# The table of chunks ahead of the feature loads, biases loaded from ScalarE's queue, and side steps spread over a whole sum

## The reference, cut to what matters

```python
agg = segment_sum(h_src[src], dst); out = elu((agg * norm_dst) @ weight + bias)      # L0
h = relu(gcn_conv(x, ...)); z = h @ W_lin + b_lin                                    # L1
out = relu(z @ W_dec1 + b_dec1) @ W_dec2 + b_dec2
h = prelu(hconv(x, W1, b1)); h = prelu(hconv(h, W2, b2) + x)                         # L2
# hconv: xt = x @ W; m = segment_sum(xt[src], dst) * Binv; segment_sum(m[dst], src) * Dinv + b
x = m @ W_gc + b_gc + feats @ W_res + b_res; y = x + moe_ff(x)   # L3: top 2 of 64 experts
```

## Time and profile before

| | us |
|---|---|
| median of 3 runs (2074.12 to 2080.96) | 2080.48 |
| the profiled execution, its own time | 2079.78 |
| its span in the trace | 2078.0 |

### The profile page before, as it was taken

One profiled execution on the slowest core, in us unless ns is written; L12 is line 12 of the kernel. 1 busy time (PEld: TensorE's weight loads), 2 busy tenths in 40 slices (PEclk: granted clock), 3 DMA queues, 4 the chain that ended last, 5 costly groups with the idle time before them and its releaser, 6 DMA issues. The chain is left out here.

```text
span 2078.0 us, 34276 instructions
## 1 busy us (share of the span) xinstructions
PE 1805.9 (87%) x9529; PEld 1435.1 (69%) x9563; DVE 887.5 (43%) x2701; ACT 498.2 (24%) x1301; POOL 492.1 (24%) x858
## 2 busy tenths in 40 slices
PE   1988886799989999999989999989999599999830
PEld 0355555688778878877768878867777498888720
DVE  4876664444434421122221127756666221212145
ACT  0034444322223311111111111111111123232252
POOL 1012222411111100000000002216666633333244
PEclk8999998899999999999999999999999799999955
DMA  5168999999868868866658888878875599999931
GB/s 127 32 234 289 319 320 342 322 323 321 269 222 268 265 198 293 288 221 219 209 185 287 290 264 292 289 235 249 265 253 181 199 376 376 375 376 374 360 127 62
DMA packets 279214, 545.09 MB, mean 262 GB/s; under 512 B 18214, under 2 KB 201040, under 8 KB 275920
## 3 DMA queue, kind: packets, MB, share of 16 engines
q1 hardware_dynamic: 271088, 526.38, 76.4%
q0 software_dynamic: 8032, 17.60, 2.3%
HBM read 415.19 MB, written 128.72 MB: 262 GB/s over the span
## 5 line engine op out<-in xcount | busy, mean ns | idle before, releaser
L1061 PE MATMUL psum<-xsa,blk 128*128 128x512 f32 x2500 | 638.9, 404 | 17.7 <-DVEq L381 8.2
L1061 PEld LDWEIGHTS psum<-xsa,blk 128*128 128x128 f32 x2500 | 460.3, 190 | 105.8 <-issue 10.6
L1061 PE MATMUL psum<-xsb,blk 128*128 128x512 f32 (+1 forms) x1875 | 416.0, 369 | 6.7 <-DVEq L381 6.0
L1061 PEld LDWEIGHTS psum<-xsb,blk 128*128 128x128 f32 x1875 | 321.7, 190 | 65.3 <-issue 7.1
L1826 POOL TENSOR_SCALAR ve<-mv 128x1 f32<-128x1 f32 x75 | 16.7, 223 | 819.6 <-DVE mv L1537 819.6
L1422 DVE TENSOR_SCALAR onehots<-counts_scratch 128x348 bf16<-128x348 f16 x464 | 161.6, 373 | 82.1 <-issue 41.6
L963 PE MATMUL psum<-onehots 128*128 128x349 bf16 x464 | 149.2, 322 | 40.5 <-DVE onehots L1427 38.3
L547 PE MATMUL psum<-route,expert_weights 128*128 128x128 f32 x1360 | 170.5, 279 | 0.1
L966 PE MATMUL psum<-zrow 128*128 128x512 bf16 x431 | 164.4, 390 | 0.0
L547 PEld LDWEIGHTS psum<-route,expert_weights 128*128 128x128 f32 x1360 | 161.0, 194 | 1.4 <-DVE route L659 0.5
L557 PE MATMUL psum<-expert_weights,route 128*128 128x256 f32 x672 | 159.8, 381 | 0.0
(11 more groups left out here) (309 smaller groups left out, 2077.1 us busy)
## 6 DMA issues: line engine op xcount, KB each, us to landing
blk<-counts_src_on_rows SPq DMA_DIRECT2D x125, 832.0 KB, 5.2
blk<-counts_src_on_rows SPq DMA_DIRECT2D x125, 768.0 KB, 4.9
expert_weights<-in_L_gnn_w SPq DMA_DIRECT2D x176, 512.0 KB, 6.0
blk<-counts_dst_on_rows SPq DMA_DIRECT2D x50, 832.0 KB, 4.4
counts_dst_on_rows<-band_rows SPq DMA_DIRECT2D x25, 1600.0 KB, 8.1
blk<-counts_dst_on_rows SPq DMA_DIRECT2D x50, 768.0 KB, 4.2
counts_src_on_rows<-blk SPq DMA_DIRECT2D x13, 1600.0 KB, 8.6
counts_src_on_rows<-rblk SPq DMA_DIRECT2D x12, 1600.0 KB, 9.8
```

What stands on the lines that cost most here:

```text
L1061: mm = e.matmul(o, blk[n][:, k * P:(k + 1) * P], XS[:, k, :, 0:Fw], start=(k == 0), stop=(k == T - 1 and not own))
```

## The change

Three edits. SP meets the "load" barrier right after the edge lists are in, ahead of the loads of X, the weights and b1. Thirteen bias loads leave SP's queue: `load_biases` issues them on ScalarE, between its two barriers; SP only counts them. And the distance between side steps is no longer limited to 8.

```diff
+        def load_biases(e):
+            lot = [(bc[w][:, :], A[k].rearrange("(a f) -> a f", a=1).to_broadcast([P, F]))
+                   for w, k in (("l0", "L0_gnn_bias"), ("dec2", "L1_gnn_b_dec2"), ("h1", "L2_gnn_b1"), ("h2", "L2_gnn_b2"),
+                                ("gc", "L3_gnn_b_gc"), ("res", "L3_gnn_b_res"), ("gam", "L3_gnn_gamma"),
+                                ("bet", "L3_gnn_beta"))]
+            lot += [(bgb[:, :], A["L3_gnn_bg"].rearrange("(a f) -> a f", a=1).to_broadcast([P, NE])),
+                    (col["conv"][:, :], A["L1_gnn_b_conv"].rearrange("(p a) -> p a", a=1)),
+                    (col["lin"][0:HL, :], A["L1_gnn_b_lin"].rearrange("(p a) -> p a", a=1)),
+                    (col["dec1"][:, :], A["L1_gnn_b_dec1"].rearrange("(p a) -> p a", a=1)),
+                    (col["a"][:, :], A["L2_gnn_a"].rearrange("(p a) -> p a", a=1).to_broadcast([P, 1]))]
+            if e is not None:
+                for o, i in lot:
+                    e.dma_start(o, i).then_inc(S("inputs_loaded"), 16)
+            return len(lot)
...
             e.wait_ge(ld, n[0])
             e.sem_inc(S("edges_loaded"), 1)
             e.wait_ge(S("pads_set"), 3)
+            phase_end(e, "load")
             load(X[:, 0:T - 1, :], x[0:(T - 1) * P, :].rearrange("(t p) f -> p t f", p=P))
...
-            for w, k in (("l0", "L0_gnn_bias"), ...):
-                load(bc[w][:, :], A[k].rearrange("(a f) -> a f", a=1).to_broadcast([P, F]))
             load(b1rows[:, :], A["L3_gnn_b1"])
-            load(bgb[:, :], ...)
-            load(col["conv"][:, :], ...)   # and lin, dec1, a
+            n[0] += 16 * load_biases(None)
...
-            phase_end(e, "load")
             phase_end(e, "table")
...
-                    gap = min(8, (T - 1) // max(len(side), 1))
+                    gap = (T - 1) // max(len(side), 1)
...
         @block.scalar
         def _(e):
             phase_end(e, "load")
+            load_biases(e)
             phase_end(e, "table")
```

More of the change, by code:

```diff
@@ L803, in _ @@
                 load(w[:, :], A[k])
-            for w, k in (("l0", "L0_gnn_bias"), ("dec2", "L1_gnn_b_dec2"), ("h1", "L2_gnn_b1"), ("h2", "L2_gnn_b2"),
-                         ("gc", "L3_gnn_b_gc"), ("res", "L3_gnn_b_res"), ("gam", "L3_gnn_gamma"),
-                         ("bet", "L3_gnn_beta")):
-                load(bc[w][:, :], A[k].rearrange("(a f) -> a f", a=1).to_broadcast([P, F]))
             load(b1rows[:, :], A["L3_gnn_b1"])
[L809 to L813, removed]
+            n[0] += 16 * load_biases(None)
             def zero_rows(buf, c, n):
```

## The result

The changed kernel took 2048.64 us in the median of its first four runs (2042.93 to 2054.5), the kernel before 2078.27 beside it; the ratio is 0.9849, interval 0.9831 to 0.9866. The forecast was 43 us faster, 2037, with 2045 as the upper end. The direction was right, the size was not. The program's own scatter is not small beside the miss: two later sets of runs of the same kernel had medians of 2043.1 and 2047.1, and the first of them lies inside the forecast's range.

A forecast was written before the change was run, and what follows sets the result against it. TensorE, busy 87% of the span, was taken as the bound, so gains lay where it stood still: 21.5 (barrier) + 21 (h1b) + 0.9 (l0) = 43.4 us, giving 2037 us, range 2030 to 2045.

The forecast's parts named there:

- The table's start and length: Chunk table on DVE: starts at 8.44 us in place of 29.91, takes 18.32 and ends at 26.76.
- I take nothing, since the nearest rows leave SP 2.3 us and ScalarE 11 us of room: Barrier after the table: ScalarE's 13 issues cost nothing, SP being through at 24.46 us, ahead of DVE.
- the upper bound of that paragraph: Barrier after the table: SP's and ScalarE's lists take turns, the last issue ends at 31.78, 5.0 us later than DVE.
- rival A: Table's end barrier: SP's and ScalarE's issues hold each other up, up to 5.0 us less gain, about 2042; chance 0.14.
- h1b: Pass h1b: later side steps remove TensorE's wait for G, 0.88 us a tile, 21 us in all.
- Rival B: Pass h1b: residual waits of 0.3 us at turn or dense step, gain 14 in place of 21, 2044; chance 0.08.
- l0: Second tile of l0: four more matmuls ahead of the turn take 0.9 us of its wait for G.
- The other stages keep their lengths: All stages but start and h1b: unchanged; one growing by more than 2 us makes the forecast wrong.
- rival D: First bands: low TensorE clock lasts longer, 0.47 us more a chunk; at 120 chunks slower, 2092; chance 0.02.
- The loads were hidden: Loads beside the table end by 40 us, 30 us before the first band store; h1b's block loads stay hidden.
- Rival C: One part gives nothing, bands bound by something unmoved or h1b by its loads: 2057 or 2058; chance 0.04.
- Rival E: Whole run: no change within 0.3%, by a mixture of part failure and low clock; chance 0.02.

The follow-up runs named there:

- e5_act_after_sp: e3_early_signal, with ScalarE also waiting to issue its 13 bias loads until SP has issued its whole list; 2043.5 us in one profiled run.
- e3_early_signal: Changed kernel, but SP and ScalarE signal the table's end barrier before issuing their loads and wait for all five behind them; 2040.27 us, ratio 0.9817.
- e7_best: e3_early_signal with the old step limit of 8 outside h1b, and h1b's turn after k = 13, dense step after k = 23; 2041.99 us, ratio 0.9805.
- e2_no_gap: Changed kernel with the old limit of 8 on the side-step distance, so barrier and biases alone; 2062.55 us, ratio 0.9927 to the kernel before.
- e6_h1b_alone: Changed kernel with the old side-step limit of 8 everywhere but in h1b; 2043.52 us, ratio 0.9825 to the kernel before.
- e4_biases_on_sp: Changed kernel with the 13 bias loads back in SP's list behind the barrier, none on ScalarE; 2042.22 us, ratio 0.9814 to the kernel before.
- e11_signal_sp_only: e3_early_signal with all load issues left on SP and ScalarE untouched; 2041.63 us, ratio 0.9807 to the kernel before.

## Why the forecast was wrong, step by step

In the two profiled executions the forecast's 43.4 us became 32.1.

- **The table's start and length: right.** 8.38 and 26.63 us; forecast 8.44 and 26.76.
- **The step that failed: "I take nothing, since the nearest rows leave SP 2.3 us and ScalarE 11 us of room".** The price of ScalarE's issues was the upper bound of that paragraph, not the lower. SP reached the barrier at 31.5, and rival A (5.0 us less) came true: the first band starts 49.87 - 33.54 = 16.33 us earlier, not 21.47, which is 5.1 us less. ScalarE itself was in time, at 22.2. The room was counted for two lists that don't touch; alone, SP would even have had 3.8 us (22.86 against 26.62 in e5_act_after_sp). That run shows that the lists hold each other up, and e3_early_signal that only the barrier passed this on. The rule of the Trainium skill, DMA: Bandwidth & Descriptors, section "Queues, rings and completion order" (a ring each, but no descriptor generator of their own), agrees with this; the runs show that something is shared, not what it is.
- **h1b: right in mechanism, 1.8 us too large.** 19.2 us in place of 21. TensorE's own work in a tile is 6.83, not 6.71, and stays so with the turn two matmuls later (e7_best). The term put at nothing is the change from the sum matmuls to the turn, 0.18 us; the turn itself was 0.05 cheaper than its 0.19. A tile saves 0.80 in place of 0.88. Rival B's residual waits did not appear.
- **l0: 0.6 in place of 0.9**, 198.4 to 197.8 between the first sums of l0 and l1. The same program gave 197.8, 198.3 and 199.2 in its three profiles, so that this part's gain is not shown; that the figure came near the forecast may be luck.
- **"The other stages keep their lengths": wrong by 4.1 us.** Bands 1.4, l1 and h1a 3.3, l3 1.5 longer; h2a 0.2 and what follows l3 1.9 shorter. TensorE's waits behind the first band's start hardly changed (the largest growth is 1.6 us, for Xn at line 1108, in the sparse end of l1). At the start of h1a it is 2.8 us at 1.2 GHz, as shown above. In l3 the first 30 us show a lower clock too, 0.89 in the kernel before (the first line) and 0.83 in the changed one (the second), as do its last 30 (0.99 and 0.94):

```profile
1375.40:1405.40 30.00, 22.27 (x100) 18.31 (x101) 13.36 (x49) 3.70 (x9) 1.99 (x5) 0.89 0.60 192
...
1343.70:1373.70 30.00, 22.26 (x94) 18.13 (x95) 12.22 (x44) 3.71 (x10) 1.99 (x5) 0.83 0.57 181
```

This is rival D's mechanism in a small size and at other places than the first bands. The bands' 1.4 us is less than the 5 us by which they vary with the program unchanged, and no cause is shown for it.

- 5.1 + 1.8 + 0.3 + 4.1 = 11.3, which is the whole miss of these two profiles.
- The loads were hidden, as forecast. Rival C (one part gives nothing) was wrong for both parts: each gave 17 us alone. Rival E (no change) was wrong too.

**What stays open.** l1 and h1a together took 309.6 to 309.9 us in three programs (before, e2_no_gap, e6_h1b_alone) and 312.8 to 313.0 in all others, and neither the distance in l1 (e7_best has the old one) nor in h1b (e6_h1b_alone has the new one) separates them. Why the low clock falls where it does stays open with it. l3 took 232.8 and 232.9 in the two programs with the old h1b and 233.9 to 234.4 in all others; the windows above show where in l3 the low clock lay, but why it lay there was not tried.

## What to carry to other kernels

A barrier waits for the engine that has nothing to do in the stage as well: if all it does there is issue transfers, let it give its signal first and wait later. Loads moved to a second engine's queue do not shorten the list when both issue at once; count the two lists as one. And a side step belongs where its input is ready: the distance between steps can be read off the time from the sum's end to that input.

## What the runs showed of the hardware

- Issues of SP and ScalarE hold each other up fully: 14.5 and 7.9 us alone, 23.2 and 13.9 side by side. The Trainium skill, DMA: Bandwidth & Descriptors, says in its section "Issuing engines are not separate DMA queues" that issuing from several engines at once saves only the sequencer's time of issuing. Here even that was not saved: the last load was issued at 29.9 to 32.0 in the eight profiles with two issuers, and at 30.6 and 30.4 with all of them on SP (e4_biases_on_sp, e11_signal_sp_only).
- The time of an issue did not go by the bytes: wcv (128 KB), wgc (256 KB) and wgt (64 KB), with 256 rows each, took 0.71, 0.71 and 0.72 us.
- The same program spreads over 13 us (2041.2 to 2054.5 in 15 runs), and its three profiles over 5 us in the band stage alone. The time goes with TensorE's mean granted clock: 0.945 to 0.946 in the six fastest of the 15 runs (up to 2043.6), 0.939 to 0.940 in the three slowest (from 2051.0).
